# The class token's steps behind remainders two groups ahead, finished images ahead of expert pieces, the last router and ranks behind down products

## The reference

```python
xb = 2.0 * jnp.pi * xyz[..., None] * freq_bands            # 6 bands
feat = jnp.concatenate([jnp.sin(xb), jnp.cos(xb)], -1).reshape(b, n, -1)
h = jnp.einsum('bnf,of->bno', feat, W)                      # 6912 features -> 192
h = concatenate([cls_tok, h], axis=1)                       # 1 class token + 512 tokens

# attention (elu+1 features, forget gates, running sums), on layernorm(h)
log_f_cum = clip(cumsum(log(sigmoid(x @ Wf + bf))), -20, 20)
num, den  = causal sums of q, k, v weighted by exp(+-log_f_cum)
h = h + (layernorm(num / den) * gamma + beta) @ Wo

# experts, on x = layernorm(h)
gates, idx = top_k(softmax(x @ router_w), 2)                # 2 of 8 experts
routed = sum_e gates_e * (silu(x @ w_gate_e) * (x @ w_up_e)) @ w_down_e
shared = (silu(x @ ws_gate) * (x @ ws_up)) @ ws_down
alpha = sigmoid(x @ sg_w + sg_b)
h = h + alpha * shared + (1 - alpha) * routed
```

## Time and profile before

| what | value |
|---|---|
| time, median of 3 runs | 561.92 us (560.88 to 562.1) |
| profiled execution | 560.57 us, of which 558.7 us are the span |
| PE busy | 536.0 us (96% of the span) |
| DVE busy | 366.0 us (66%) |
| ACT busy | 306.2 us (55%) |
| POOL busy | 188.1 us (34%) |
| chain of waits | PE 81%, DVE 12%, ACT 4%, issue 2% |
| granted TensorE clock, mean | 0.994 of full |

### The profile page before, as it was taken

One profiled execution on the slowest core, in us unless ns is written; L12 is line 12 of the kernel. 1 busy time (PEld: TensorE's weight loads), 2 busy tenths in 40 slices (PEclk: granted clock), 3 DMA queues, 4 the chain that ended last, 5 costly groups with the idle time before them and its releaser, 6 DMA issues.

```text
span 558.7 us, 9144 instructions
## 1 busy us (share of the span) xinstructions
PE 536.0 (96%) x3251; PEld 504.3 (90%) x3251; DVE 366.0 (66%) x1034; ACT 306.2 (55%) x418; POOL 188.1 (34%) x212
## 2 busy tenths in 40 slices
PE   9999876999999999999999999999898999999997
PEld 9999766989999989999989999978777899999875
DVE  8845665743856963988763996467897356666537
ACT  4482536997475785865787664364242134455410
POOL 6243352122234312484311480002600414444410
PEclk9999998999999999999999999999999999999999
DMA  8900049001010000130000010511103441531164
GB/s 326 332 30 19 20 142 304 26 0 29 1 38 20 2 19 11 39 95 2 1 0 11 20 50 9 174 53 29 57 2 114 131 161 51 165 100 55 52 209 145
DMA packets 23489, 42.49 MB, mean 76 GB/s; under 512 B 2503, under 2 KB 15045, under 8 KB 23349
## 3 DMA queue, kind: packets, MB, share of 16 engines
q1 hardware_dynamic: 19560, 33.31, 18.3%
q0 software_dynamic: 3472, 8.07, 4.1%
q10 hardware_dynamic: 412, 0.53, 0.4%
HBM read 31.74 MB, written 14.79 MB: 83 GB/s over the span
## 4 chain that ended last, share of the span: by engine, by line
PE 81%; DVE 12%; ACT 4%; issue 2%; ACTq 0%; DVEq 0%
PE ps L1486 35%; PE ps L1482 5%; PE ps L1730 4%; PE ps L1484 2%; PE ps L1783 2%; PE ps L1785 2%; DVE feat L910 2%; PE ps L1692 2%; PE ps L1696 1%; PE ps L1694 1%; PE ps L1695 1%; PE ps L1693 1%; PE ps L1761 1%; PE ps L1762 1%; PE ps L1763 1%
## 5 line engine op out<-in xcount | busy, mean ns | idle before, releaser
L1486 PE MATMUL ps<-w_tok,feat 128*128 128x192 f32 x1392 | 236.6, 330 | 10.5 <-ACT H L590 4.3
L1486 PEld LDWEIGHTS ps<-w_tok,feat 128*128 128x128 f32 x1392 | 229.4, 192 | 12.5 <-issue 12.3
L449 POOL TENSOR_SCALAR feat<-fx 128x512 int32<-128x512 f32 x108 | 93.5, 881 | 152.4 <-PE ps L1484 104.6
L910 DVE SCALAR_TENSOR_TENSOR feat<-fx,feat 128x512 f32<-128x512 f32 x102 | 73.1, 770 | 2.4 <-POOL feat L449 2.2
L557 ACT ACTIVATE feat<-feat 128x1536 f32<-128x1536 f32 x34 | 50.5, 1485 | 31.4 <-DVE feat L917 30.6
L554 ACT ACTIVATE feat<-feat 128x1536 f32<-128x1536 f32 x27 | 40.0, 1483 | 41.5 <-DVE feat L910 41.5
L495 POOL DMA_INDIRECT ydram<-yr,xs x39 | 37.9, 972 | 53.9 <-DVE yr L1249 53.9
L560 ACT ACTIVATE feat<-feat,half_pi 128x1536 f32<-128x1536 f32 x35 | 54.6, 1559 | 0.0
L1482 PE MATMUL ps<-w_r,X 128*128 128x384 f32 x168 | 52.0, 375 | 0.0
L692 ACT ACTIVATE s_ring<-ps 128x512 f32<-128x512 f32 x24 | 14.4, 598 | 53.5 <-PE ps L1696 53.5
L489 POOL DMA_INDIRECT slots<-pay_a,posi x17 | 17.4, 1021 | 76.7 <-DVE posi L1175 73.3
(11 more groups left out here) (322 smaller groups left out, 991.8 us busy)
## 6 DMA issues: line engine op xcount, KB each, us to landing
slots<-in_blank SPq DMA_DIRECT2D x1, 5031.0 KB, 18.9
w_tok<-in_wT SPq DMA_DIRECT2D x7, 576.0 KB, 9.2
fx<-in_xT SPq DMA_DIRECT2D x15, 256.0 KB, 2.7
xs<-slots SPq DMA_DIRECT2D x5, 645.0 KB, 6.0
yin<-ydram SPq DMA_DIRECT2D x8, 384.0 KB, 6.6
raw_a<-in_wea SPq DMA_DIRECT2D x4, 384.0 KB, 5.2
raw_b<-in_web SPq DMA_DIRECT2D x4, 384.0 KB, 6.1
w_tok<-in_wT SPq DMA_DIRECT2D x4, 288.0 KB, 7.7
```

What stands on the lines that cost most here:

```text
L449: ins = pool.tensor_scalar(feat[:, k % SLOTS, i, :].bitcast(I32), x[:, x_block(k), :], f_col[:, fi:fi + 1], 1.0, ALU.mult, ALU.mult)
L910: ins = dve.scalar_tensor_tensor(feat[:, s, i, :], x[:, x_block(k), :], f_col[:, fi:fi + 1], feat[:, s, i, :].bitcast(I32), ALU.mult, ALU. ...
L1486: return pe.matmul(out_, feat[:, k % SLOTS, i, tokens], w_tok[:, w_at(k) + i, :], start=(k == 0 and i == 0), stop=(k == NG - 1 and i == 5) ...
```

## The change

Three things are moved; no instruction is changed.

1. During image 0, DVE's `remainders` and ACT's `sines` stand one class-token step earlier, so that they are two groups ahead. The class token's router leaves image 0 and goes to the place in image 1 where the other images' routers stand, on TensorE, DVE and ACT; `gates(0)` moves with it.
2. In the shared expert, `finish(0)` moves from ahead of `hidden(8)` to behind `hidden(7)`, ahead of two expert pieces, and `finish(1)` from ahead of `hidden(14)` to ahead of `hidden(13)`.
3. On TensorE the two halves of `router(B)` and `ranks(B)` move behind `down`: the first half behind `down(9)`, the second behind `up_one(12, 0)`, the ranks behind `down(10)`.

```diff
@@ ACT, image 0 @@
             weight_high(4)
+            sines(0, 7)
             attn6(0)
             split_hi_piece(0)
-            sines(0, 7)
             weight_high(5)
+            sines(0, 8)
             split_hi_piece(1)
-            sines(0, 8)
             weight_high(6)
+            sines(1, 0)
             attn8(0)
-            sines(1, 0)
             weight_high(7)
-            router(0)
             take_h(0)
@@ ACT, images 1 to 3 @@
-                if b >= 2:
-                    router(b - 1)
+                router(b - 1)
@@ DVE, image 0 @@
             remainders(0, 5)
+            remainders(0, 6)
             attn3(0)
             make_state()
             attn5(0)
-            remainders(0, 6)
+            remainders(0, 7)
             attn6(0)
             split_piece(0)
-            remainders(0, 7)
+            remainders(0, 8)
             attn7(0)
             split_piece(1)
-            remainders(0, 8)
+            remainders(1, 0)
             attn8(0)
             dve.wait_ge(split_done, SP_)
             dve.memset(spare[0:DB, 0, :], 0.0)
-            remainders(1, 0)
-            router(0)
@@ DVE, images 1 to 3 @@
                 attn0(b)
-                if b == 1:
-                    gates(0)
                 remainders(b, 2)
                 attn1(b)
-                if b >= 2:
-                    router(b - 1)
+                router(b - 1)
                 remainders(b, 3)
                 negatives(b)
                 clip_odds(b)
-                if b >= 2:
-                    gates(b - 1)
+                gates(b - 1)
@@ DVE, shared expert @@
-                if q in (NCS + 2, 2 * NCS + 2):
-                    finish(q // NCS - 1)
+                if q == 2 * NCS + 1:
+                    finish(1)
                 hidden(q)
+                if q == NCS + 1:
+                    finish(0)
@@ TensorE, images @@
             pe.wait_ge(router_split, 2)
-            router(0, 0)
-            router(0, 1)
 
             for b in range(1, B):
                 project(b, 0, range(3))
-                if b >= 2:
-                    router(b - 1, 0)
+                router(b - 1, 0)
                 project(b, 0, range(3, 6))
                 attn1(b)
-                if b >= 2:
-                    router(b - 1, 1)
+                router(b - 1, 1)
@@ TensorE, shared expert @@
+                if q == Q_LG + 1:
+                    router(B, 1)
                 up_one(q, 1)
...
+                if q >= 2:
+                    down(q - 2)
                 if q == Q_LG:
                     router(B, 0)
                 if q == Q_RK:
                     ranks(B)
-                if q >= 2:
-                    down(q - 2)
-                if q == Q_LG:
-                    router(B, 1)
```

## The result

| | before | changed kernel |
|---|---|---|
| median | 561.4 us (560.63 to 562.1) | 547.93 us (547.31 to 548.59) |
| ratio | | 0.9761, 95% interval 0.9739 to 0.9783 |
| profiled execution, span | 560.57, 558.7 us | 548.59, 546.8 us |
| PE busy | 536.0 us (96%) | 534.0 us (98%) |
| DVE, ACT, POOL busy | 366.0, 306.2, 188.1 us | 363.8, 303.2, 193.9 us |

(Medians of four executions each.) The kernel is 2.4% faster: 13.5 us by the medians, 12.0 by the two profiled executions. Three executions that took very much longer (782 us of the kernel before, 1406 and 913 us of b3_rem_first) are left out of all medians and ratios here.

The account below looks back on a forecast made before the run. It took TensorE, busy nearly all the time, as the bound, so its waits and slow clock were to go: 13.8 + 1.4 = 15.2 us off the 561.92 median gives 546.7; own range 545.3 to 547.8, 8-in-10 range 544.8 to 550.3.

Parts of the forecast that it names:

- The waits for features, and the slow clock: Around image 0's last groups: TensorE's waits for ACT (10.44 us, including 4.28 for H) and 3.36 us of slow clock go.
- The rival that put the slow group down to the transfer: DMA transfer, not idle time, stretched the matmuls of the slow groups, so 3.36 us stay: 549.9 us; chance 6%.
- From group 8 into image 1 with no wait: End of image 0: TensorE goes on without waiting for ACT's copies of H, as the router is no longer in between.
- The margin of 1.8 us: Image 1's group 0: ACT starts copying H at 79.5, first copy wanted at 81.7; tightest margin of all.
- Zero for the copy of k: Image 1: the router's 3.6 us on DVE cost TensorE's transposes of k nothing; flight and margin share 3.3 us.
- its 13.8: Forecast gain in image 0: 10.44 us of waits plus 3.36 us of slow clock, at worst 10.2.
- given back in image 1: Rival, 20%: late copies of H or k in image 1 lose half of 3.6 us (548.3) or all (550.1).
- the slow groups stay slow: Rival, 6%: the blank transfer at DMA share 0.99 stretched the matmuls, so 3.36 us stay: 549.9 us.
- Finished images: Shared expert, chunk 7: finish(0) runs unheld beside POOL in 1.39 us, the 1.45 us wait at down(6) goes; worth 1.3 us.
- the other reading, held for 4 us: Shared expert: finish(0) is held by POOL like the expert pieces, ends at 403.3, and half a microsecond of wait stays.
- Router and ranks behind down: 0.1 in all: Last image's router and ranks: new waits of 0.6 and 0.85 us; 1.4 us with the finished images, 0.1 of it here.
- Without the idle stretches nothing lowers the clock: Group 8 and image 1's group 0: both take 8.04 us instead of 9.72 once TensorE's waits are gone.

Follow-up runs that it names:

- b3_rem_first: Changed kernel with DVE's remainders(1, 0) put ahead of split_piece(1) instead of behind it; 544.74 us, ratio 0.9714.
- a1_image0: Kernel before with the image 0 part alone: features two groups ahead, class token's router moved into image 1; 548.88 us, ratio 0.978.
- a4_tail: Kernel before with the shared expert's moves alone: finish(0) and finish(1) earlier, router(B) and ranks(B) behind down; 558.88 us, ratio 0.9954.
- b2_no_finish_move: Changed kernel with finish(0) and finish(1) put back ahead of hidden(8) and hidden(14); 549.33 us, ratio 0.9796.
- a3_router: Kernel before with only the class token's router and gates moved into image 1, features left in place; 554.52 us, ratio 0.9883.

## Why the prediction was right, and where it was not

- **The waits for features, and the slow clock.** Right: groups 7 and 8 without a bracket, 7.97 to 8.07 us, clock 1.00. Group 8 was foretold as wanted at 73.8; it started at 73.56. The rival that put the slow group down to the transfer fell (DMA share 0.98, 7.97 us).
- **"From group 8 into image 1 with no wait".** This is the step that failed, and the prediction's own sign for it ("if ACT's copies of `H` still end a wait of 1 us or more") came true. The margin of 1.8 us was spent, and 1.31 us more. The layout had the second split piece end at 72.3 and the remainders at 74.4. They ended at 74.16 and 77.45: DVE was 0.8 us late at the end of `attn7(0)` (70.67 for 69.9), the piece waited 0.86 more for ACT, and that moved the remainders into POOL's rounds, where they took 3.26 us instead of 2.05. For the 0.86 us the layout had no term, though the row of before has 1.27 at the same place. The 0.8 us begin with the change itself: with the sines of group 6 sooner, ACT does its weight piece `weight_high(4)` at 49.75 in place of 58.44, POOL's piece that waits for it comes at 50.34 in place of 59.03, and there it holds DVE's layernorm for 0.82 us (last section). `remainders(0, 7)` starts at 53.23 for a forecast 52.50, and what follows is late with it. The copies of `H` came at 82.37 for a forecast 79.5. I had counted that contention (up to 1.5) against the margin, and alone it would have fitted; I had not counted it together with the delay ahead of it, which is what brings it about. b3_rem_first shows it from the other side: with the remainders ahead of the piece neither the 0.86 nor the 1.2 us arises, and the wait is gone.
- **Zero for the copy of k.** Wrong by 0.77 us. In the rows of before the issue led the transposes by 133.28 - 129.54 = 3.74 us, and the after shows 2.28 from issue to a start that waited, so the margin was 1.5 and not up to 3.3. DVE's router took 94.89 to 97.33, 2.4 us and not 3.6. 1.31 and 0.77 make 2.1 us; image 0 fell short of its 13.8 by 1.8 at the transposes of k (11.98) and by 2.0 by the medians of a1_image0 (11.8). The rival "given back in image 1" was thus true for over half of its 3.6 us, and the changed kernel lies between it and my forecast. (The prices of this rival and of "the slow groups stay slow" are each 0.2 us too low for the sum they start from: 546.7 and 1.8, 3.6 or 3.36 give 548.5, 550.3 and 550.1.)
- **Finished images.** `finish(0)` beside POOL took 1.39 us, as the Trainium skill's rule would have it (SBUF — State Buffer, "Who interferes with whom"); the other reading, held for 4 us, is excluded. It brought 1.39 us by a4_tail, foretold 1.3.
- **Router and ranks behind down: 0.1 in all.** The sum was near (1.56 for both parts in a4_tail, foretold 1.4), but of two terms that I had not parted. `finish(1)` ahead of `hidden(13)` gives 0.6 (20.36 in a1_image0 to 19.76), and the router's halves cost 0.43. The waits came as foretold: 0.42 at the ranks (foretold 0.6) and 0.74 for `silu(12)` (0.85); `down(12)` waits 0.50, half of its 1.09 before.
- **The total.** 15.2 us were foretold and 13.5 measured by the medians. The faster pair of the changed kernel's executions, 547.3, is 13.3 below the profiled 560.57; the two waits make up the 2 us that are missing, and the slower pair is 1.2 us longer, which the last section puts down to the clock. The measured 547.93 lies just above the forecast's own range (545.3 to 547.8) and inside the wide one (544.8 to 550.3). That 546.7 came within 1.2 us is in part luck: the median of before that it started from, 561.92 of three executions, is 1.2 above what later sets gave, and that hid half of the miss.
- **"Without the idle stretches nothing lowers the clock".** True of the two groups that it was said of, and false as a general sentence: see the last section.

## What to carry to other kernels

Delays in a chain laid out by hand are not to be held against a margin one by one: a step that slips may slip into another engine's work on the same memory and slip again. Where two steps share one engine's list, ask which of them someone waits for; here the split piece was wanted by nobody for long, and putting it behind the remainders was worth another 2.5 us at no cost. And a product that starts a long chain (the logits) belongs ahead of one that fills time, even if it waits a moment itself.

## What the runs showed of the hardware that was not expected

**A lower clock with TensorE never idle.** Changed kernel, TensorE, at the start of chunk 1; ahead of these rows stand ten products of 128x10, five `up_one` products and ten products of 128x10 again.

```profile
346.23 0.25 PE L1662 MATMUL ps<-wrb,X 128*128 128x10 f32 x1
346.34 0.69 PE L1687 MATMUL ps<-X,wa_hi 128*128 128x512 f32 x1
...
349.82 0.42 PE L1690 MATMUL ps<-X,wb 128*128 128x512 f32 x1
350.07 0.39 PE L1691 MATMUL ps<-X,wb 128*128 128x512 f32 x1
```

The window of that stretch:

```profile
346.00:350.00 4.00, 4.00 (x14) 3.26 (x14) 3.55 (x21) 0.11 (x1) 0.00 (x0) 0.57 1.02 372
```

From 346.34 to 350.07 it is 3.73 us for nine products, which took 2.18 in the kernel before (358.28 to 360.46), and the granted clock of the stretch is 0.57, near the 1.2 GHz level. TensorE had not waited. The same order of products stands in the kernel before and in the other ten traces, and the nine products take 2.2 us in each; so it happens in some executions and not in others. It took 1.55 us there, and TensorE's lead falls from 11.94 us ahead of it to 10.63 at 368.00; the two pairs of times lie 1.2 apart, with a mean clock of 0.997 in the slower and 0.999 and 1.00 in the faster. That the faster pair lacks this stretch is a conclusion from these numbers, since neither of its executions has a profile. In b2_no_finish_move it happened at the other place with that order, the one that part 3 makes at chunk 12 (windows of that kernel):

```profile
408.00:410.00 2.00, 2.00 (x15) 1.81 (x15) 0.55 (x2) 0.00 (x0) 0.00 (x0) 1.00 0.30 55
410.00:412.00 2.00, 2.00 (x6) 1.52 (x6) 1.69 (x10) 0.00 (x0) 0.00 (x0) 0.51 0.93 359
```

There it cost next to nothing: `attn8` to `down(12)` took 20.78 us, a1_image0's 20.36 and the 0.43 of part 3, as far as the rows tell because DVE's chain ended that stretch and the slow products filled what had been waits (no bracket at the ranks and at `up_one(13, 1)` there). What starts the low clock in one execution and not in the next was not settled. Both times a DMA share over 0.9 lay beside it, but in the kernel before the share from 358 to 362 is 1.00 at a clock of 1.00.

**A wait of 2 us, with and without a slow group behind it.** In the kernel before the group behind 2.03 us of wait ran at clock 1.00 in 8.04 us; in a3_router the group behind 2.04 us took 9.72, at 0.79 from 66 to 74, and the next one, behind 2.28 us, 8.04. Behind 1.31 us it stayed 1.00 (changed kernel), behind 3.97 and 4.28 us it was 0.82 in both groups (kernel before).

**Small instructions are held too.** One two-element instruction of DVE's layernorm in image 0 took 0.97 us when POOL's weight piece had just begun, where its like take 0.15; both ended within 0.02 us of one another. In the kernel before, with no piece of POOL beside it, the same instruction took 0.15. This is where the 0.8 us of delay in image 0 began (changed kernel, DVE):

```profile
50.38 0.97 DVE L880 SCALAR_TENSOR_TENSOR ya<-y 2x1 f32<-2x1 f32 x1
...
51.75 0.15 DVE L880 SCALAR_TENSOR_TENSOR ya<-y 2x1 f32<-2x1 f32 x1
```

POOL:

```profile
50.34 1.00 POOL L460 TENSOR_TENSOR w_r<-w_tok,w_r 128x384 fp32r<-128x384 f32 x1 [0.53 <-ACT w_r L567]
```
